# A two-layer language-model tower: where the gathered expert outputs of each sequence land

## The chip, the cores and the metric

The kernel runs on one core of a Trainium2 chip. The metric is the device time of one execution in microseconds. Before the change it is 443.67 us, the median of 3 runs (443.1 to 444.18).

## The reference, cut to what matters

Four sequences of 512 tokens go through an embedding, an attention and a feed-forward layer (layer 0), a second attention and a mixture of experts (layer 1). The end of the last layer is what the change touches:

```python
probs = jax.nn.softmax(xf @ gate_w, axis=-1)
dispatch_w, expert_idx = jax.lax.top_k(probs, 2)
combine = jnp.sum(jax.nn.one_hot(expert_idx, E) * dispatch_w[..., None], axis=1)
for e in range(8):
    h = jax.nn.gelu(xf @ w1[e] + b1[e], approximate=False)
    y = h @ w2[e] + b2[e]
    out = out + combine[:, e:e + 1] * y
return x + out.reshape(B, S, D)          # D = 128, hidden width 512
```

## The kernel before, in words

Everything is fp32. A sequence is 4 tiles of 128 tokens by 128 channels; the residual stream of all 16 tiles stays in SBUF (`h`). The kernel computes an expert only for the tokens that chose it. POOL scatters each token's row to its two experts' regions in DRAM (`dealt`), SP loads full tiles of 128 rows of one expert back, PE multiplies them, SP stores the results (`experts_out`), and POOL gathers for each token its two result rows, which DVE adds to `h` with their weights.

Work is cut into sections with a letter, a number and a phase, written X5.0 or K30.3. T, A, B, C, O are embedding and first attention of a sequence, D, H, E its first feed-forward layer, F the preparation of the second attention (linear layers, cumulative decays by scans on DVE), G its 16 blocks, I normalisation and gating, R ranking and scattering, Z the tables of tiles (group 0: sequences 0 to 2, group 1: half of sequence 3). V loads expert weights. X loads a batch of up to 4 dealt tiles, Q transposes it. K is one of 42 tiles of tokens (0 to 30 group 0, 31 to 41 group 1): K.0 on DVE copies the expert's two weight matrices to `w1s` and `w2s` (L1708, L1710; three buffers each), K.1 is the up matmul (L1049), K.2 GELU on ACT (L1262), K.3 the down matmul (L1057), K.4 the copy out of PSUM on DVE (L1713). W stores a batch of results (L574; W0 to W7 group 0, W8 to W10 group 1). J computes the last half of sequence 3 densely, for all 8 experts: J.0 up (L1012), J.1 GELU (L1272), J.2 down (L1020), J.3 add on DVE (L1614). Y0.0 on POOL gathers the result rows of a sequence (`section_Y`, L731; 8 gathers of 128 rows, 4 for sequence 3), Y.1 on DVE adds them (L1725), U stores a sequence to `out` (L588).

Each engine runs its own list of sections from the table `ORDER`, in exactly that order; semaphores alone tie the lists together. So a section that waits holds up all that stands behind it on its engine. PSUM has 8 banks; 7 of them go round as a ring in the order of PE's table, and each matmul group waits until the bank's last content has been read (`room`).

All gathers of Y land in one buffer, `yg`, which is laid over `qkv` of the first attention. So `section_Y` waits for the last matmul that reads `qkv` (C.pe.kv of sequence 3) and for the last add of the sequence before:

```python
wait(pool, "C.pe.kv", B - 1)
wait(pool, "Y.dve.b3", b - 1)
```

The end of DVE's list is `... K35.0 K36.0 Y0.1 K33.4 K34.4 K37.0 K38.0 K39.0 K35.4 K36.4 J2.3 J3.3 K40.0 Y1.1 K37.4 K41.0 K38.4 K39.4 K40.4 K41.4 J4.3 Y2.1 J5.3 J6.3 J7.3 Y3.1`.

Of the kernel before, what the change touches and what calls it, by code (L numbers as in the profile page):

```python
# [5 lines left out]
ALU = mybir.AluOpType  # L6
# [8 lines left out]
B, S, D = 4, 512, 128  # L15
T = S // P
# [15 lines left out]
LEAD = 3  # L32
# [92 lines left out]

ORDER = {
    "sp": (
        "V0.0 V1.0 V2.0 V3.0 V4.0 V5.0 V6.0 V7.0 X0.0 X1.0 X2.0 X3.0 X4.0 X5.0 X6.0 X7.0 X8.0 X9.0 X10.0 W0.0 "
        "W1.0 W2.0 W3.0 W4.0 W5.0 W6.0 W7.0 W8.0 W9.0 U0.0 U1.0 W10.0 U2.0 U3.0"),
    "pool": (  # L130
# [20 lines left out]
    "act": (  # L151
# [12 lines left out]
    "dve": (  # L164
# [16 lines left out]
}  # L181


def lm_tower(nc, a, out):
# [5 lines left out]
    with ctx:  # L190
# [11 lines left out]
        def wait(eng, step, b):  # L202

            if b >= 0:
                eng.wait_ge(sem[step.rsplit(".", 1)[0]], count(step, b))
# [93 lines left out]
        la = sb("la", [P, PAIRS, S])  # L299
# [54 lines left out]
        blk = sb("blk", [P, D + HEADS0])  # L354

        qkv = sb("qkv", [P, T, 3 * D + 1])
        yg = qkv[:].rearrange("p t c -> p (t c)")[:, 0:2 * T * D].rearrange("p (k t c) -> p k t c", k=2, t=T)
        sq = sb("sq", [P, T, 2 * D])
        amp = sq
        n2 = few("n2", [P, 4, T * 16])  # L360
# [13 lines left out]
        vv = sb("vv", [P, T, HEADS1 * HD1])  # L374
        lb = sb("lb", [P, PAIRS, S])
        kk, qq = la, lb
        zeros = lb[:].rearrange("p a b -> p (a b)")

        big = sb("big", [P, 2 * E * FF])
# [215 lines left out]
        def _(pool):  # L595
# [125 lines left out]
            def section_Y(b, ph):  # L721
                if ph == 0:
                    g = b // LEAD
                    wait(pool, "Z.dve.pi", g)
                    pool.wait_ge(s_ys[g], 16 * sum(x[0] == g for x in BATCHES))
                    wait(pool, "C.pe.kv", B - 1)
                    wait(pool, "Y.dve.b3", b - 1)
                    for t in range(PART[b]):
                        for k in range(2):
                            at = b % LEAD * T + t  # L730
                            pool.indirect_dma_start(  # L731
                                yg[:, k, t, :], None, ys[g],
                                bass.IndirectOffsetOnAxis(ap=posi[g][:, k, at:at + 1], axis=0)).then_inc(s_yg[b], 16)

            each("pool", {"A": section_A, "B": section_B, "O": section_O, "D": section_D, "H": section_H,
# [544 lines left out]
        def _(dve):  # L1280
# [434 lines left out]
            def section_Y(b, ph):  # L1715
                if ph == 1:
                    dve.wait_ge(s_yg[b], 16 * 2 * PART[b])
                    wait(dve, "R.dve.w", b)
                    wait(dve, "I.dve2.h", b)
                    for t in range(PART[b]):  # L1720
                        hb = h[:, b * T + t, :]
                        for k, name in enumerate("ab"):
                            if k:
                                wait(dve, "Y.dve.a%d" % t, b)
                            did(dve.scalar_tensor_tensor(hb, yg[:, k, t, :], wts[b // LEAD][:, b % LEAD * T + t, k:k + 1], hb, ALU.mult, ALU.add),  # L1725
                                "Y.dve.%s%d" % (name, t), b)

            each("dve", {"T": section_T, "A": section_A, "B": section_B, "C": section_C, "O": section_O,
# [86 lines left out]
```

## Time and profile before

| | before |
|---|---|
| median of 3 runs | 443.67 us (443.1 to 444.18) |
| the profiled execution | 443.62 us, span 441.5 us |
| mean granted TensorE clock | 0.956 |
| PE busy | 388.5 us (88%) |
| DVE busy | 311.1 us (70%) |
| ACT busy | 213.0 us (48%) |
| POOL busy | 135.9 us (31%) |
| gathers of expert outputs, POOL L731 | 28, mean 964 ns |

The busy shares are means over the whole span: the first 100 us, the end and a short stretch near 280 us leave PE idle, the rest is full. Engines are told apart as PE (matmul), PEld (its weight loads), DVE, ACT, POOL and SP; a `q` behind a name is the engine's queue of commands. In a timeline the idle time of the engine before an instruction stands in brackets, with what ended it. A row that groups several matmuls of one kind (x8) shows the time from the first to the modelled end of the last, which overlaps the next group a little.

### The profile page before, as it was taken

What the parts mean: (1) busy time and instruction counts of PE and PEld (TensorE: products, weight loads), DVE (VectorE), ACT (ScalarE), POOL (GpSimd) and SP (SyncE); (2) the same over time, 40 slices, a digit from 0 to 9 for tenths busy, and PEclk for the clock granted to TensorE, in tenths of its full rate; (3) what the DMA queues carried; (4) which work ended last, traced back from release to release, by engine and by line L of the source; (5) the groups of instructions that cost most, each with busy time, mean ns of one, the idle gap of its engine ahead of it and who ended that gap; (6) DMA issues with size and microseconds to landing.
All of it is one profiled execution on the core that took longest, in us unless ns stands there. A gap on an engine that the chain in (4) does not pass through costs nothing.

```text
span 441.5 us, 8913 instructions
## 1 busy us (share of the span) xinstructions
PE 388.5 (88%) x2864; PEld 305.2 (69%) x2864; DVE 311.1 (70%) x989; ACT 213.0 (48%) x456; POOL 135.9 (31%) x139
## 2 busy tenths in 40 slices
PE   2557859998999999999999999689999999999590
PEld 1334738575549875598655884368999999998590
DVE  1478798788999867999799659994377655517332
ACT  1228474953663743722346227213679466774230
POOL 6771214152403012014146027350011100065443
PEclk9996697999999999999999999899999999999896
DMA  5899500000000000000047000012220141111232
GB/s 157 321 377 423 240 0 2 1 1 0 1 1 1 1 1 1 2 1 2 0 143 286 2 1 31 19 48 57 60 57 25 50 132 49 45 49 55 62 94 71
DMA packets 24021, 31.71 MB, mean 72 GB/s; under 512 B 4377, under 2 KB 18720, under 8 KB 22696
## 3 DMA queue, kind: packets, MB, share of 16 engines
q1 hardware_dynamic: 21416, 25.63, 16.5%
q0 software_dynamic: 2560, 5.52, 4.4%
q8 instruction: 23, 0.38, 0.3%
q14 instruction: 22, 0.18, 0.1%
HBM read 18.16 MB, written 12.98 MB: 71 GB/s over the span
## 4 chain that ended last, share of the span: by engine, by line
PE 53%; DVE 17%; issue 14%; POOL 7%; DMA 5%; ACT 3%; POOLq 0%; DVEq 0%
PE bank L923 5%; POOL qkv L731 5%; PE bank L952 4%; PE bank L975 4%; PE bank L936 3%; PE bank L890 3%; PE bank L870 3%; PE bank L884 3%; PE bank L960 3%; PE bank L1049 2%; PE bank L968 2%; PE bank L917 2%; PE bank L908 2%; DMA qkv<-experts_out,arena 2%; DVE h L1725 2%
## 5 line engine op out<-in xcount | busy, mean ns | idle before, releaser
L1262 ACT ACTIVATE arena<-bank,arena 128x128 f32<-128x128 f32 x168 | 47.9, 370 | 40.1 <-PE bank L1049 39.9
L1057 PE MATMUL bank<-w2s,arena 128*128 128x128 f32 x336 | 46.0, 282 | 0.7 <-DVE fs L1713 0.7
L731 POOL DMA_INDIRECT qkv<-experts_out,arena x28 | 27.0, 964 | 63.6 <-issue 48.5
L1057 PEld LDWEIGHTS bank<-w2s,arena 128*128 128x128 f32 x336 | 42.4, 197 | 1.3 <-DVE fs L1713 0.9
L717 POOL DMA_INDIRECT dealt<-xy,arena x28 | 29.2, 1042 | 32.7 <-DVE arena L1649 25.2
L923 PE MATMUL bank<-xT_f,wq 128*128 128x512 f32 x64 | 30.5, 621 | 0.7 <-DVE vv L1508 0.7
L1710 DVE COPY w2s<-big 128x512 f32 x42 | 18.4, 437 | 16.2 <-PE bank L1057 16.1
L1708 DVE COPY w1s<-big 128x512 f32 x42 | 17.9, 426 | 14.2 <-PE bank L1049 9.8
L1540 DVE TENSOR_TENSOR arena<-bank,causal 128x512 f32<-128x512 f32 x32 | 20.3, 682 | 8.1 <-PE bank L936 8.1
L923 PEld LDWEIGHTS bank<-xT_f,wq 128*128 128x128 f32 x64 | 12.3, 198 | 15.3 <-issue 12.7
L1725 DVE SCALAR_TENSOR_TENSOR h<-qkv,arena,h 128x128 f32<-128x128 f32 x28 | 9.0, 349 | 19.5 <-DMA qkv<-experts_out,arena 19.1
L1049 PE MATMUL bank<-arena,w1s 128*128 128x128 f32 x160 | 21.3, 277 | 0.0
L1519 DVE TENSOR_TENSOR_SCAN lb<-la 128x512 f32<-128x512 f32 x16 | 20.5, 1283 | 0.0
L708 POOL TENSOR_TENSOR arena<-arena 128x8 f32<-128x8 f32 x4 | 6.8, 1690 | 41.9 <-DVE arena L1554 41.9
L1049 PEld LDWEIGHTS bank<-arena,w1s 128*128 128x128 f32 x160 | 19.4, 192 | 0.3 <-issue 0.2
L1215 ACT ACTIVATE arena<-bank 128x512 f32<-128x512 f32 x12 | 7.0, 596 | 24.9 <-PE bank L944 24.9
L689 POOL TENSOR_TENSOR arena<-arena 128x4 f32<-128x4 f32 x4 | 4.2, 1061 | 47.5 <-DVE arena L1299 47.5
L1220 ACT ACTIVATE arena<-bank 128x512 f32<-128x512 f32 x16 | 9.5, 596 | 18.5 <-PE bank L960 17.3
L936 PE MATMUL bank<-lb,la 64*128 64x128 f32 x256 | 18.3, 284 | 0.0
L952 PE MATMUL bank<-arena,vv 128*64 128x128 f32 x256 | 17.5, 279 | 0.9 <-DVE arena L1540 0.9
L599 POOL DMA_INDIRECT arena<-in_tables,idx x16 | 16.5, 1031 | 5.8 <-issue 4.4
L936 PEld LDWEIGHTS bank<-lb,la 64*128 64x128 f32 x256 | 15.5, 187 | 2.3 <-issue 1.5
(280 smaller groups left out, 1000.3 us busy)
## 6 DMA issues: line engine op xcount, KB each, us to landing
dealt<-lb SPq DMA_DIRECT2D x7, 1024.0 KB, 13.3
big<-in_tv SPq DMA_DIRECT2D x2, 2048.0 KB
big<-in_ew SPq DMA_DIRECT2D x16, 256.0 KB, 5.9
arena<-dealt SPq DMA_DIRECT2D x20, 64.0 KB, 1.8
experts_out<-arena SPq DMA_DIRECT2D x5, 256.0 KB, 3.0
wq<-in_wq SPq DMA_DIRECT2D x1, 1024.0 KB, 18.1
out<-h SPq DMA_DIRECT2D x4, 256.0 KB, 3.0
u<-dealt SPq DMA_DIRECT2D x8, 64.0 KB, 1.9
```

The source lines that it names most:

```text
L717: pool.indirect_dma_start(xs[b // LEAD], bass.IndirectOffsetOnAxis(ap=goal[b][:, k, t:t + 1], axis=0), xy[b % 2][:, t, :], None).then_inc( ...
L731: pool.indirect_dma_start(yg[:, k, t, :], None, ys[g], bass.IndirectOffsetOnAxis(ap=posi[g][:, k, at:at + 1], axis=0)).then_inc(s_yg[b], 16)
L923: did(pe.matmul(p[:], wq[:, at * 512 + j * P:at * 512 + (j + 1) * P], xT_f[:], start=True, stop=True), "F.peq.%s%d" % (name, j), b)
L936: last = pe.matmul(half[m][:, j * P:(j + 1) * P], kk[rows, j, tk], qq[rows, j, tk], start=True, stop=True)
L952: last = pe.matmul(p[m * HD1:(m + 1) * HD1, j * P:(j + 1) * P], vv[:, c, (2 * j + m) * HD1:(2 * j + m + 1) * HD1], sim[k][:, m, j, :], sta ...
L1049: last = pe.matmul(p[:, c * P:(c + 1) * P], w1s[n % WAYS][:, c * P:(c + 1) * P], tiles(g, j, 1)[:, 0, :], start=True, stop=True)
L1057: last = pe.matmul(p[:, 0:D], hid[n % 2][:, c * P:(c + 1) * P], w2s[n % WAYS][:, c * D:(c + 1) * D], start=(c == 0), stop=(c == FC - 1))
L1262: last = act.activation(hid[n % 2][:, c * P:(c + 1) * P], of("K.up", n)[:, c * P:(c + 1) * P], ACT.Gelu, bias=eb1[:].rearrange("p e c -> p ...
L1519: did(dve.tensor_tensor_scan(lb[:, j, :], la[:, j, :], la[:, j, :], 0.0, ALU.add, ALU.bypass), "F.dves.sum%d" % j, b)
L1540: did(dve.tensor_tensor(sim[n % 2][:, m], of("G.qk%d" % m, n)[:].rearrange("p (a b) -> p a b", a=PAIRS), causal[:].unsqueeze(1).to_broadca ...
L1708: did(dve.tensor_copy(w1s[n % WAYS][:], big[:, bass.ds(e * FF, FF)]), "K.dve.w1", n)
L1710: did(dve.tensor_copy(w2s[n % WAYS][:], big[:, bass.ds(e * FF + E * FF, FF)]), "K.dve.w2", n)
```

## The change

`yg` becomes a list of four buffers, one for each sequence. Sequence 0 keeps the place in `qkv`; 1 and 2 get the two halves of `vv` (the values of the second attention), 3 gets half of `la` (its keys). POOL no longer waits for the adds of the sequence before. Sequence 0 waits for C.pe.kv as before, the others for the last output projection of the second attention (G.pe3.out of block 15). DVE reads `yg[b]`. All five tables of `ORDER` are made anew: each engine has the same sections as before, in another order.

```diff
-        yg = qkv[:].rearrange("p t c -> p (t c)")[:, 0:2 * T * D].rearrange("p (k t c) -> p k t c", k=2, t=T)
+        yg = [x.rearrange("p (k t c) -> p k t c", k=2, t=T) for x in (
+            qkv[:].rearrange("p t c -> p (t c)")[:, 0:2 * T * D], vv[:].rearrange("p t c -> p (t c)")[:, 0:2 * T * D],
+            vv[:].rearrange("p t c -> p (t c)")[:, 2 * T * D:], la[:].rearrange("p a b -> p (a b)")[:, 0:2 * T * D])]
...
-                    wait(pool, "C.pe.kv", B - 1)
-                    wait(pool, "Y.dve.b3", b - 1)
+                    if b == 0:
+                        wait(pool, "C.pe.kv", B - 1)
+                    else:
+                        wait(pool, "G.pe3.out", B * T - 1)
...
-                                yg[:, k, t, :], None, ys[g],
+                                yg[b][:, k, t, :], None, ys[g],
...
-                            did(dve.scalar_tensor_tensor(hb, yg[:, k, t, :], wts[b // LEAD][:, b % LEAD * T + t, k:k + 1], hb, ALU.mult, ALU.add),
+                            did(dve.scalar_tensor_tensor(hb, yg[b][:, k, t, :], wts[b // LEAD][:, b % LEAD * T + t, k:k + 1], hb, ALU.mult, ALU.add),
```

Of the tables, the parts that the prediction speaks of, old and new:

```diff
     "sp": (
-        ... X5.0 X6.0 X7.0 X8.0 X9.0 X10.0 W0.0 W1.0 ... W8.0 W9.0 U0.0 U1.0 W10.0 U2.0 U3.0
+        ... X5.0 W0.0 W1.0 X6.0 X7.0 W2.0 X8.0 X9.0 X10.0 W3.0 ... W9.0 W10.0 U0.0 U1.0 U2.0 U3.0
     "pe": (
-        ... F0.3 O2.4 F0.7 E1.0 F0.15 F0.23 F0.31 E1.1 F0.13 F0.21 F0.29 F0.5 F0.37 E1.3 G0.2 G1.2 G0.0 ...
+        ... F0.3 O2.4 F0.7 F0.15 F0.23 F0.31 F0.13 E1.0 E1.1 F0.21 F0.29 F0.37 F0.5 G0.0 E1.3 G1.0 G0.2 ...
-        ... G11.8 R1.1 F3.3 F3.7 ... F3.37 G12.2 G13.2 G12.0 G12.5 G14.2 G13.0 G13.5 G12.4 ...
+        ... R1.1 G10.4 I1.9 ... G11.8 F3.3 I1.11 F3.7 ... F3.37 I2.9 G12.2 G13.2 G12.0 I2.11 G13.0 G12.5 G14.2 G12.4 ...
-        ... K13.3 K15.1 Q6.0 ...
+        ... K13.3 K14.1 K15.1 Q6.0 Q7.0 ...
-        ... Q8.0 K23.3 ... K29.3 K31.1 K30.3 K32.1 K31.3 Q9.0 Q10.0 K33.1 K32.3 K34.1 J2.0 J3.0 K33.3 K35.1 K34.3
-        K36.1 J2.2 J3.2 K35.3 K36.3 K37.1 K38.1 J4.0 K37.3 K39.1 K38.3 J5.0 K40.1 K39.3 K41.1 K40.3 K41.3 J4.2 J6.0
-        J5.2 J7.0 J6.2 J7.2
+        ... K29.3 Q8.0 Q9.0 K30.3 K31.1 Q10.0 J2.0 K32.1 J3.0 J2.2 K31.3 K33.1 K32.3 K34.1 K33.3 K35.1 K34.3 K36.1
+        K35.3 K37.1 K36.3 K38.1 K37.3 K39.1 J3.2 K38.3 K40.1 K39.3 K41.1 K40.3 J4.0 J5.0 K41.3 J4.2 J5.2 J6.0
+        J7.0 J6.2 J7.2
     "act": (
-        T0.1 T0.4 T0.6 T1.1 B0.0 B0.2 T1.4 B0.4 B0.6 T1.6 T2.1 C0.1 T2.4 B1.0 B1.2 T2.6 B1.4 O0.3 T3.1 B1.6 ...
+        T0.1 T0.4 T0.6 T1.1 T1.4 B0.0 B0.2 B0.4 B0.6 T1.6 T2.1 C0.1 B1.0 T2.4 B1.2 B1.4 T2.6 T3.1 O0.3 B1.6 ...
     "dve": (
-        ... A1.0 T2.2 C0.1 A1.4 T3.0 B1.1 B1.3 C0.3 B1.5 O0.0 T3.2 A2.0 B1.7 ...
+        ... A1.0 T2.2 T3.0 A1.4 C0.1 B1.1 B1.3 C0.3 B1.5 O0.0 T3.2 A2.0 B1.7 ...
-        ... F3.38 I2.12 Z0.0 G12.1 ...
+        ... F3.38 Z0.0 G12.1 I2.12 ...
-        ... K36.0 Y0.1 K33.4 K34.4 K37.0 K38.0 K39.0 K35.4 K36.4 J2.3 J3.3 K40.0 Y1.1 K37.4 K41.0 K38.4 K39.4 K40.4
-        K41.4 J4.3 Y2.1 J5.3 J6.3 J7.3 Y3.1
+        ... K30.4 K32.0 K33.0 K34.0 K35.0 J2.3 K36.0 K31.4 K32.4 K33.4 K34.4 K37.0 K38.0 K35.4 K39.0 Y0.1 K40.0
+        K36.4 K37.4 K38.4 K41.0 K39.4 J3.3 K40.4 K41.4 Y1.1 J4.3 Y2.1 J5.3 J6.3 J7.3 Y3.1
```

## Rows read from the trace of the kernel before

**Rows 1.** spans and granted clock: span in us, mean TensorE clock

```profile
core 0: 441.5 us, clock 0.956
```

**Rows 2.** waits from 380 us: waiter <- releaser, total us, times, longest

```profile
DVE h L1725 <- DMA qkv<-experts_out,arena: 19.1, 4, 5.6
...
POOL qkv L731 <- DVE h L1725: 15.1, 3, 5.1
...
PE bank L1049 <- DVE w1s L1708: 4.6, 1, 4.6
```

**Rows 3.** timeline, gathers and sums: start, duration us, engine, what, [idle before <-releaser]

```profile
385.94 0.99 POOL L731 DMA_INDIRECT qkv<-experts_out,arena  x1 [41.20 <-issue]
...
394.90 0.95 POOL L731 DMA_INDIRECT qkv<-experts_out,arena  x1 [0.31 <-issue]
...
397.37 2.69 DVE L1725 SCALAR_TENSOR_TENSOR h<-qkv,arena,h 128x128 f32<-128x128 f32 x8 [4.36 <-DMA qkv<-experts_out,arena]
...
400.45 0.43 DVE L1708 COPY w1s<-big 128x512 f32 x1
...
400.83 1.21 POOL L731 DMA_INDIRECT qkv<-experts_out,arena  x1 [4.99 <-DVE h L1725]
...
436.89 1.39 DVE L1725 SCALAR_TENSOR_TENSOR h<-qkv,arena,h 128x128 f32<-128x128 f32 x4 [4.98 <-DMA qkv<-experts_out,arena]
```

**Rows 4.** windows: length, busy PE PEld DVE ACT POOL, clock, DMA share, GB/s

```profile
382.70:400.00 17.30, 16.89 (x137) 16.28 (x135) 6.43 (x20) 10.65 (x33) 7.77 (x8) 1.00 0.15 43
...
400.00:416.00 16.00, 11.13 (x80) 10.18 (x80) 8.49 (x28) 6.03 (x20) 8.00 (x9) 1.00 0.18 51
...
416.00:431.30 15.30, 15.18 (x104) 14.60 (x104) 5.60 (x20) 5.96 (x16) 8.11 (x9) 0.89 0.39 108
...
431.30:441.50 10.20, 0.00 (x0) 0.00 (x0) 1.92 (x6) 0.00 (x0) 3.10 (x4) 0.62 0.23 63
```

**Rows 5.** timeline where group 0's last tile leaves

```profile
382.90 0.29 DVE L1713 COPY fs<-bank 128x128 f32<-128x128 f32 x1 [0.76 <-PE bank L1057]
...
383.22 0.36 SPq L574 DMA_DIRECT2D experts_out<-fs  x1
```

**Rows 6.** chain of waits, the expert stage: start, duration us, what

```profile
334.23 0.89 PE bank L1049 x8
...
335.12 1.73 PE bank L1012 x8
```

**Rows 7.** timeline of the front, DVE and PE

```profile
57.26 1.21 DVE L1366 TENSOR_REDUCE arena<-sq 128x64 f32<-128x1024 f32 x1
...
67.22 1.23 DVE L1388 TENSOR_TENSOR fs<-sq,fs 128x1024 f32<-128x1024 f32 x1
...
83.85 3.64 PE L870 MATMUL bank<-big,arena 128*32 128x512 f32 x32
```

**Rows 8.** timeline, DVE reading the bank of q0

```profile
125.73 0.74 DVE L1526 SCALAR_TENSOR_TENSOR lb<-bank,arena,lb 128x512 f32<-128x512 f32 x1
```

**Rows 9.** timeline of sequence 3's second attention, PE and DVE

```profile
264.17 0.64 PE L900 MATMUL bank<-ident,xn_f 128*128 128x128 f32 x4
...
290.13 0.68 DVE L1604 TENSOR_TENSOR h<-h,bank 128x512 f32<-128x512 f32 x1
...
297.14 1.09 PE L952 MATMUL bank<-arena,vv 128*64 128x128 f32 x16 [0.93 <-DVE arena L1540]
```

**Rows 10.** PE's longest waits from 110 to 380 us: total us, times, longest

```profile
PE bank L995 <- DVE arena L1601: 3.1, 1, 3.1
...
PE bank L944 <- DVE la L1530: 1.1, 1, 1.1
```

**Rows 11.** timeline, SP's loads of dealt rows; DVE's copy of K7

```profile
297.84 22.30 SPq L569 DMA_DIRECT2D arena<-dealt  x20
...
331.60 0.48 DVE L1713 COPY arena<-bank 128x128 f32<-128x128 f32 x2
```

**Rows 12.** timeline, POOL's slowest indirect DMA

```profile
284.94 1.62 POOL L717 DMA_INDIRECT dealt<-xy,arena  x1 [6.37 <-DVE arena L1649]
```

More of the change, by code:

```diff
@@ L127 @@
     "sp": (
-        "V0.0 V1.0 V2.0 V3.0 V4.0 V5.0 V6.0 V7.0 X0.0 X1.0 X2.0 X3.0 X4.0 X5.0 X6.0 X7.0 X8.0 X9.0 X10.0 W0.0 "
-        "W1.0 W2.0 W3.0 W4.0 W5.0 W6.0 W7.0 W8.0 W9.0 U0.0 U1.0 W10.0 U2.0 U3.0"),
+        "V0.0 V1.0 V2.0 V3.0 V4.0 V5.0 V6.0 V7.0 X0.0 X1.0 X2.0 X3.0 X4.0 X5.0 W0.0 W1.0 X6.0 X7.0 W2.0 X8.0 X9.0 "
+        "X10.0 W3.0 W4.0 W5.0 W6.0 W7.0 W8.0 W9.0 W10.0 U0.0 U1.0 U2.0 U3.0"),
     "pool": (
[2 rows of a table removed]
[2 rows of a table added]
         "F3.3 I2.1 R1.3 R2.3 I3.1 R3.3 Y0.0 Y1.0 Y2.0 Y3.0"),
```

90 rows, old and new, of the table ORDER are left out of this document.

## The prediction

> **What bounds the kernel now.** I read the span and clock first: 441.5 us at a mean granted clock of 0.956 [rows 1]; the same execution took 443.62 us, so 2.12 us lie outside the span. It stands 0.05 us under the median of 443.67 us, so the sum below is made against 443.62 and needs no correction.
>
> Next, the waits of the last 61 us [rows 2]. POOL waits 15.1 us in three pieces for the weighted sums of line 1725, and DVE waits 19.1 us in four pieces for gathers to land. That is a ring: one buffer `yg` serves all four sequences, so the gathers of sequence b+1 (POOL) start only when step Y1 of sequence b (DVE) has read it. The timeline shows one turn [rows 3]: first gather at 385.94, eighth at 394.90, DVE adds from 397.37 to 400.06, next gather at 400.83. From the eighth gather to the next sequence's first are 400.83-394.90 = 5.93 us, where a gather otherwise follows the last in 1.25 to 1.28 (7 intervals in 8.96 us). Three turns lose 3 x (5.93-1.28) = 14 us.
>
> TensorE is the other half. It is busy 16.89 of 17.3 us, then 11.13 of 16.0, then 15.18 of 15.3 at a clock of 0.89 [rows 4], and ends at 431.3. The middle hole is PE waiting 4.6 us for a `w1s` copy [rows 2] that stands behind Y1 in DVE's queue, itself waiting for a gather. So the new end is not found by subtracting 14 us: when the ring is gone, PE's own work is late next, and I rebuild the tail from that.
>
> **The change, part by part.**
>
> *Start of the tail.* The last tile of group 0, K30, is copied out at 382.90 and its store goes out on SP at 383.22 [rows 5]; the gathers start at 385.94, 3.0 us after the copy. K30's down matmuls ended 0.2 before it, at 382.70. In the new PE table the same work precedes K30.3 but for K31.1 (out, 0.89) and Q9.0 (in, 0.44), so K30.3 ends 0.45 earlier, at 382.25, and the first gather starts at 385.5.
>
> *PE's remaining work.* After K30.3 the new table has 11 K.up and 11 K.down, each 0.89, and six J.up at 1.73 [rows 6]; six J.down with 16 matmuls of K's shape each, twice 0.893, 1.79; and one Q10 of about 0.35. Sum: 22 x 0.893 + 6 x 1.73 + 6 x 1.79 + 0.35 = 41.1 us. Without a stall PE ends at 423.4, against 431.3. The clock was 1.00 in the first stretch and 0.89 after the hole [rows 4]; without the hole I take 1.00.
>
> *Does DVE stall it?* I walked DVE's new list against PE's. Y0.1 comes when K39.0 is copied, about 399.9; the gathers landed at 385.5 + 7 x 1.28 + 2.5 = 397.0 (2.5 is 397.37-394.90), so it waits for nothing, and takes 2.69 [rows 3] until 402.6. Behind it stand K40.0 (needed by K40.1 at 404.9, ready 403.0) and K41.0 (needed 406.7, ready 405.6). Both have over 1 us to spare: no stall. If the gathers came 2 us later than 399.9, this cover is gone.
>
> *POOL.* The three waits for Y.dve.b3 go; the wait for G.pe3.out is met with G15.8, ahead of K2.3 in PE's order and so before the matmuls of rows 6, and costs nothing. 24 gathers at up to 1.28 put the last start of sequence 2 at 385.5 + 23 x 1.28 = 414.9, landed 417.4. K41.3 ends at 412.8 (423.4 less 2 J.up, 4 J.down, 3.46 + 7.16 = 10.6), its store lands about 415.9. Sequence 3's four gathers start then and land at 422.3.
>
> *End.* DVE: Y1.1 413.1 to 415.8, J4.3, Y2.1 417.4 to 420.1, J5.3, J6.3, then J7.3, which needs PE's last matmul, to 424.1. Y3.1 takes 1.39 to 425.5. From the end of that step to the span's end are now 441.5-438.28 = 3.2 us [rows 1, 3]. New span: 428.7. The tail gives 441.5-428.7 = **-12.8 us**. On SP, W10 moves ahead of U0 and U1, whose waits for Y then hold nothing up.
>
> *The tables ahead of the tail* also change, with the same instructions. I followed what differs.
> - Front: DVE does T3.0 before A1.4, not between A1.4 and B1.1. The reduction of B1.1, now at 57.26 [rows 7] and kept from its input, can go 1.9 us earlier. The scalar work T2.6 and T3.1 in between leaves about 0.9 of it at step B1.7 (67.22). T1.4, placed ahead of B0.0 on ACT, delays sequence 0 by about 0.3. PE becomes dense at 83.85 [rows 7], and all that stands behind it moves by the rest: **-0.6**.
> - F of sequence 0: F0.13 now comes before E1.0. With a ring of seven banks, the matmul k1 of F0.21 takes the bank of q0, which DVE reads at 125.73 (0.74 us) [rows 8]. PE, dense here before, reaches it at about 124.6 and waits: **+1.2**. I found no such case for the other three sequences.
> - F of sequence 3: I1.11 (0.9 us) leaves the work ahead of F3.3, which starts at 264.17, and I2.12 (0.68) moves behind G12.1 on DVE [rows 9]. G12.1 ends 1.6 earlier; its waiter G12.4 (297.14) can follow, but 1.09 of matmuls (G13.5) are then still to do: **-0.5**.
> - What I didn't follow: bounds 0 and 4.2, the two longest PE waits of the stretch from 110 to 380 [rows 10], should new ones of that size appear. PE showed almost none in its dense stretch, so I take the value near zero: **+0.6**. Below zero there is little, as PE is full there.
> - SP: X6 and X7 now stand behind W1. Twenty such loads take 22.30 us [rows 11], so seven take 8, after W1, which follows the copy of K7 at 331.6; they land at 342, and Q6.0 comes near 350. Nothing is lost.
>
> Sum: 443.62 - 12.8 - 0.6 + 1.2 - 0.5 + 0.6 = **431.5 us**.
>
> *Gathers beside DVE copies.* The gather at 400.83, with a DVE copy that began at 400.45 and others behind it, took 1.21 us where the one at 394.90 took 0.95 [rows 3]; I allowed for that with 1.28. The Trainium skill ("SBUF — State Buffer", "SBUF: two separate sides") speaks against the change: a DMA issued by GpSimd can't write its descriptors while VectorE runs a copy from SBUF to SBUF, which holds the shared port. The copies of `w1s` and `w2s` are such. By its figures ("A bandwidth-pool intuition that's wrong") a DMA of 620 ns becomes one of 3100 ns; if every gather did, its stream would end past 470 us. That is an estimate from the page; the rows show a tenth of that effect.
>
> **Rivals.**
> 1. *The tables cost more.* The dense stretch is given up in places for a short tail. Price: the 4.2 us bound in place of 0.6, 435.1 us; the range for it is 433.5 to 437.5. For: the bank wait above. Against: no dependency changed there. Chance 0.20.
> 2. *The ring goes, but DVE still waits at Y0.1 or PE at a late copy*, as now [rows 2]. One 4.6 us wait returns: 436.1 us, and up to the bounds of "same". Chance 0.05.
> 3. *Slower: the gather stream becomes the bound.* If the port collisions hit each gather, it costs what the slowest indirect DMA of this kernel cost, 1.62 us [rows 12], plus the 0.30 between two. Then 28 in a row end at 385.5 + 27 x 1.92 + 2.5 = 439.8, and the time is 439.8 + 1.39 + 3.2 + 2.12 = 446.5 us. It exceeds the present time from a spacing of 1.81 us on. Most gathers show 1.25. Chance 0.03.
> 4. *The change doesn't do what it says*: ys[0] or the DVE places of Y1 hold the gathers anyway. Then about 443 us. Against: rows 2 name DVE as the releaser three times. Chance 0.02.
> 5. *More gain*: the front's 1.9 us arrives in full and nothing is lost: 443.62-12.8-1.9-0.5 = 428.4 us. Chance 0.12.
>
> The forecast (429.5 to 433.5) has 0.58. The range from 428.0 to 437.0 holds it, nearly all of rivals 1 and 5 and half of 2. Within 0.2% (0.9 us, about what a measurement of this kernel can tell from no change) lies rival 4 alone; slower is rival 3 alone. Faster 0.95, same 0.02, slower 0.03.
>
> **What would show it.** Right: 24 gathers in one run of 1.25 to 1.3 us from about 385 to 415, no POOL wait for line 1729; PE busy over 98% from 382 to 423 at a clock of 1.00; Y0.1 without a DMA wait; the last chain running through PE and J, not POOL. A PE wait of some 1 us at 124 shows the bank step, a start of PE's dense work near 83 the front. Wrong: gathers of 1.6 us or more; a PE wait over 2 us after 382; K30.3 later than 384, which would put the loss in the tables.

## The result, and the profile after

On the chip of the first comparison the changed kernel took 431.89 us (430.96 to 432.71) beside 443.43 us for the kernel before: a ratio of 0.9733, interval 0.9708 to 0.9758. The prediction was 431.5 us. On another chip it was the other way round, 461 us against 446, and kernels with the same gathers lost on two more of the four chips of the later groups. Both are told here, the first result first.

The profiled execution took 430.96 us with a span of 429.2 us at a mean clock of 0.972. The windows of the tail (us, then busy time and instruction count of each engine, clock, DMA share, GB/s):

```profile
380.00:400.00 20.00, 20.00 (x167) 19.59 (x166) 8.58 (x27) 13.70 (x43) 10.92 (x11) 1.00 0.25 70
400.00:420.00 20.00, 20.00 (x152) 19.18 (x151) 11.84 (x39) 10.51 (x31) 15.21 (x16) 1.00 0.36 103
```

Against [rows 4], PE has no hole and the clock stays at 1.00. The waits of the last 60 us (engine, what waited, releaser: us in total, times, longest), and the timeline's gathers and adds (start, us, engine, line, operation, idle before):

```profile
POOL vv L735 <- issue: 4.9, 16, 0.3
DVE h L1729 <- DMA vv<-experts_out,arena: 1.0, 1, 1.0
DVE h L1729 <- DMA la<-experts_out,arena: 0.7, 1, 0.7
```

```profile
385.73 0.98 POOL L735 DMA_INDIRECT qkv<-experts_out,arena  x1 [34.64 <-issue]
387.02 0.96 POOL L735 DMA_INDIRECT qkv<-experts_out,arena  x1 [0.31 <-issue]
...
400.38 2.68 DVE L1729 SCALAR_TENSOR_TENSOR h<-qkv,arena,h 128x128 f32<-128x128 f32 x8
...
413.37 2.70 DVE L1729 SCALAR_TENSOR_TENSOR h<-vv,arena,h 128x128 f32<-128x128 f32 x8
...
420.09 0.99 POOL L735 DMA_INDIRECT la<-experts_out,arena  x1 [0.30 <-issue]
...
423.76 0.61 DVE L1618 SCALAR_TENSOR_TENSOR h<-bank,arena,h 128x128 f32<-128x128 f32 x2 [1.18 <-PE bank L1024]
425.11 1.39 DVE L1729 SCALAR_TENSOR_TENSOR h<-la,arena,h 128x128 f32<-128x128 f32 x4 [0.74 <-DMA la<-experts_out,arena]
```

The three POOL waits for DVE are gone, and of the 19.1 us that DVE waited for gathers [rows 2] 1.7 are left. All 28 gathers stand in one run from 385.73 to 420.09, where the ring of [rows 3] stretched them to 434.37. Y0.1, at 400.38, waits for no DMA. PE's last product is done at 423.7, but the chain that ended last runs through POOL's gathers and the landing of the last one, and not through PE as the prediction's sign for "right" wanted:

```profile
420.09 5.00 DMA la<-experts_out,arena
```

### The profile page after: what moved, and what is told of

Its sections match the earlier page's. It is cut to its first block, busy times and chain, and to the rows that moved or that the text cites. A ratio compares the mean times of both kernels' runs of the same rounds, so it can differ in the third digit from the quotient of the medians.

```text
span 429.2 us, 8910 instructions
## 1 busy us (share of the span) xinstructions
PE 381.6 (89%) x2864; PEld 300.8 (70%) x2864; DVE 312.9 (73%) x989; ACT 214.2 (50%) x456; POOL 137.4 (32%) x139
## 4 chain that ended last, share of the span: by engine, by line
PE 55%; DVE 17%; issue 12%; POOL 8%; ACT 4%; DMA 3%; POOLq 0%; DVEq 0%
PE bank L1053 8%; PE bank L1061 8%; PE bank L927 3%; PE bank L979 3%; PE bank L956 3%; PE bank L894 3%; PE bank L940 2%; POOL vv L735 2%; PE bank L964 2%; DMA arena<-in_tables,idx 2%; PE bank L972 2%; POOL arena L601 2%; PE bank L874 2%; PE bank L1016 2%; PE bank L813 2%
## 5 line engine op out<-in xcount | busy, mean ns | idle before, releaser
L1061 PE MATMUL bank<-w2s,arena 128*128 128x128 f32 x336 | 44.2, 275 | 0.0
L719 POOL DMA_INDIRECT dealt<-xy,arena x28 | 31.4, 1120 | 33.7 <-DVE arena L1653 26.4
L1061 PEld LDWEIGHTS bank<-w2s,arena 128*128 128x128 f32 x336 | 41.0, 192 | 0.1
L1714 DVE COPY w2s<-big 128x512 f32 x42 | 18.0, 428 | 19.1 <-PE bank L1061 18.9
L1523 DVE TENSOR_TENSOR_SCAN lb<-la 128x512 f32<-128x512 f32 x16 | 19.5, 1218 | 2.0 <-ACT la L1205 2.0
L1219 ACT ACTIVATE arena<-bank 128x512 f32<-128x512 f32 x12 | 7.0, 594 | 25.5 <-PE bank L948 25.5
L735 POOL DMA_INDIRECT qkv<-experts_out,arena x8 | 7.7, 964 | 36.8 <-issue 36.8
L735 POOL DMA_INDIRECT vv<-experts_out,arena x16 | 15.5, 971 | 4.9 <-issue 4.9
L979 PE MATMUL bank<-wo,arena 128*128 128x128 f32 x128 | 17.0, 280 | 0.0
```

The source lines that it names most:

```text
L719: pool.indirect_dma_start(xs[b // LEAD], bass.IndirectOffsetOnAxis(ap=goal[b][:, k, t:t + 1], axis=0), xy[b % 2][:, t, :], None).then_inc( ...
L735: pool.indirect_dma_start(yg[b][:, k, t, :], None, ys[g], bass.IndirectOffsetOnAxis(ap=posi[g][:, k, at:at + 1], axis=0)).then_inc(s_yg[b] ...
L979: last = pe.matmul(p[:, 0:D], oc[k][:, j, :], wo1[:, j, :], start=(j == 0), stop=(j == PAIRS - 1))
L1061: last = pe.matmul(p[:, 0:D], hid[n % 2][:, c * P:(c + 1) * P], w2s[n % WAYS][:, c * D:(c + 1) * D], start=(c == 0), stop=(c == FC - 1))
L1523: did(dve.tensor_tensor_scan(lb[:, j, :], la[:, j, :], la[:, j, :], 0.0, ALU.add, ALU.bypass), "F.dves.sum%d" % j, b)
```

## Experiments

### The four pieces apart, and the first surprise

Two kernels separate buffers and tables, one keeps the old tables up to the tail, and one puts copies beside the gathers.

```
e1: ORDER of the kernel before; buffers and waits of the change
e2: ORDER of the change; one buffer and wait(pool, "Y.dve.b3", b - 1) of the kernel before
e3: as e1, with the new order of PE from behind K29.3, ACT from behind K30.2, DVE from behind K30.0, SP from W3.0
```

> The four buffers with the order tables of the kernel before. Theory (the ring of gather and add was the loss, and the buffers alone remove it): the first 12 gathers run as before, the next 8 follow them without a break, so Y1.1 starts near 407.5 us instead of 412.4, Y2.1 and Y3.1 wait for TensorE's last products instead of for gathers, and TensorE's work sets the end. The stall of TensorE at the weight copy behind Y0.1 in the old VectorE order stays, so the end lies 1 to 3 us behind that of the new tables: 433.7 us (432.0 to 435.5). Rival (the new tables carry the gain, the buffers only permit them): within 2 us of the kernel before, 441.5 to 443.5 us.

> The new order tables with the one buffer and the waits of the kernel before. Theory: the ring returns, and since the new VectorE order puts the adds of sequences 0 and 1 later, it is closed later than in the kernel before: the gathers of sequence 1 from about 403.8 us, Y1.1 near 415.3, the gathers of sequence 2 from 418.7, Y2.1 near 430.1, those of sequence 3 from 433.5, end near 446.5 us (444.5 to 448), slower than the kernel before by some 3 us. Rival (the tables carry the gain): 432 to 436 us.

> The four buffers with the old order tables up to the TensorE turn K29.3 and the VectorE turn K30.0, and the new order behind them. Theory: the new tables ahead of the tail are worth 0.2 to 0.5 us, since the 1.2 us they gain by 83 us are given back by 105 us; so 431.9 to 432.5 us, within 0.2% of the changed kernel. Rival (the front's gain of 1.2 us is kept to the end and the tail alone explains less): 433.1 us or more.

The fourth:

```
+    for x in [w1m[:]] + [wq[:, i * 512:(i + 1) * 512] for i in range(4)] + [
+            wo1[:].rearrange("p a b -> p (a b)"), bv1[:], w1t[:]] if n == 41 else []:
+        dve.tensor_copy(x, w2m[:])
     wait(dve, "K.pe2.down", n)
```

> The changed kernel with eight more VectorE copies of 128x512 float32 from one SBUF buffer to dead ones, ahead of the last result copy K41.4, where VectorE sat idle for 4.05 us (409.1 to 413.2) beside the gathers of sequence 2. They compute nothing that is used. By the rows of this kernel (gathers beside such copies took 1.04 to 1.26 us against 0.95) each of the three or four gathers beside them takes 0.1 to 0.3 us longer, Y2.1 starts up to 1 us later, the end moves by 0 to 0.8 us. By the rule that a gather can't write descriptors while such copies run, no gather would get through between 409.1 and 412.7: the gathers behind are all 3 us later, sequence 3's last is issued at about 423 us and the end is 2.5 to 3 us later, 434.5 us.

Measured, beside 447.43 us for the kernel before: e1 458.97 us (ratio 1.0228, 1.0185 to 1.0271), e2 456.59 (1.0209, 1.0152 to 1.0266), e3 459.58 (1.0248, 1.0212 to 1.0284), e6 462.37 (1.0318, 1.0284 to 1.0351). No expectation held, and the split between buffers and tables can't be read from these four, because all of them show something that neither first trace has. In e1, PE's timeline, with the gathers running from 385.6 on:

```profile
398.51 0.37 PE L1023 MATMUL bank<-big,ht 128*128 128x128 f32 x1 [1.06 <-issue]
399.91 0.37 PE L1023 MATMUL bank<-big,ht 128*128 128x128 f32 x1 [1.03 <-issue]
400.63 0.37 PE L1023 MATMUL bank<-big,ht 128*128 128x128 f32 x1 [0.34 <-issue]
...
406.97 0.37 PE L1023 MATMUL bank<-big,ht 128*128 128x128 f32 x1 [1.75 <-issue]
409.77 0.37 PE L1023 MATMUL bank<-big,ht 128*128 128x128 f32 x1 [2.43 <-issue]
...
418.90 0.37 PE L1023 MATMUL bank<-big,ht 128*128 128x128 f32 x1 [0.33 <-issue]
419.59 4.00 PE L1023 MATMUL bank<-big,ht 128*128 128x128 f32 x18 [0.33 <-issue]
```

These matmuls take 0.11 us each elsewhere (16 in 1.79). Here they start 0.7, 1.4, 2.1 or 2.8 us apart, in steps of 0.7, and wait for nothing that the profile shows. At 419.59, 4.8 us after the start of the 24th gather (414.82), they run back to back again, at first in 0.22 us each, since the granted clock had fallen to 0.50 while PE stood. The effect is no matter of unbroken gathers alone: e2 keeps the ring and its pauses, and still lost 9 us. In its trace the products that PE makes beside the first eight gathers (389.45 to 398.27) reach DVE and ACT only at 400.4 to 401.2 us; Y0.1, which stands behind K39.0 in the new order, comes at 410.91, and the next gathers start only at 414.37. In e6 the added copies ran only from 441.3 to 444.1, when no gather ran, so it says nothing on copies beside gathers, and that question got no answer.

### Is it the kernel or the chip?

> The changed kernel itself once more, beside the kernel before. In the four kernels of the first group the signal of a TensorE product that was done by 391 us reached VectorE and ScalarE 7 to 27 us late while GpSimd's gathers ran, and their times were 455 to 462 us. If that belongs to the chip or the moment and not to those four kernels, this one shows it too: about 456 to 459 us, with late signals between 390 and 420 us. If it belongs to the four kernels (an order or an instruction count), this one takes 431 to 433 us on the same chip.

> The kernel before itself, for its trace on the chip of the others: if the late signals belong to the chip, they show between 386 and 400 us here too, and the time is about 447 us, as it was beside the first group; if not, 443 to 444 us and no signal more than 0.5 us behind its product.

The unchanged texts of both kernels, on another chip: the changed kernel took 460.95 us (460.07 to 462.24), the kernel before 445.97 us, ratio 1.0339 (1.0311 to 1.0366); the single profile of the kernel before 445.64 us. So it isn't the four kernels. The same program that took 431.9 us takes 29 us more on this chip (456 to 459 were expected). The windows for the 35 us of the gathers, first in the first trace of the changed kernel, then here:

```profile
385.00:420.00 35.00, 35.00 (x276) 33.91 (x275) 18.16 (x58) 20.99 (x64) 26.13 (x27) 1.00 0.30 86
385.00:420.00 35.00, 15.31 (x105) 14.44 (x103) 4.46 (x12) 7.57 (x23) 23.10 (x24) 0.73 0.18 52
```

PE, busy throughout in the first trace, is busy 15.31 us. Its timeline shows how:

```profile
392.82 1.06 PE L1061 MATMUL bank<-w2s,arena 128*128 128x128 f32 x8
393.71 1.06 PE L1053 MATMUL bank<-fs,w1s 128*128 128x128 f32 x8
394.61 1.06 PE L1061 MATMUL bank<-w2s,arena 128*128 128x128 f32 x8
395.50 1.06 PE L1053 MATMUL bank<-fs,w1s 128*128 128x128 f32 x8
397.39 0.43 DVE L1714 COPY w2s<-big 128x512 f32 x1 [8.71 <-remote]
402.36 1.14 ACT L1266 ACTIVATE arena<-bank,arena 128x128 f32<-128x128 f32 x4 [9.37 <-remote]
403.64 2.04 PE L1061 MATMUL bank<-w2s,arena 128*128 128x128 f32 x8 [7.09 <-ACT arena L1266]
...
412.90 0.43 DVE L1714 COPY w2s<-big 128x512 f32 x1 [14.30 <-remote]
417.88 0.94 POOL L735 DMA_INDIRECT vv<-experts_out,arena  x1 [0.30 <-issue]
422.72 2.22 ACT L1266 ACTIVATE arena<-bank,arena 128x128 f32<-128x128 f32 x8 [19.22 <-remote]
424.01 2.05 PE L1061 MATMUL bank<-w2s,arena 128*128 128x128 f32 x8 [16.61 <-ACT arena L1266]
```

DVE's `w2s` copy at 397.39 waits for the product of PE at 392.82 alone, which its record ends at 393.9: 3.5 us late. The copy at 412.90 waits for the product at 394.61: 17 us late. ACT's step at 402.36 waits for the product recorded at 393.71, 7.6 us late, and one of the two at 422.72 for that at 395.50, 26 us late. Then everything runs again, 4.8 us after the start of the 24th gather, as in e1. PE comes back at the lower of its two clocks (granted 0.50 from 404 to 424 us): the product at 424.01 takes 2.05 us, where one at full clock takes 1.06. "remote" stands where the page finds no releaser on this core. Whether PE itself was slow, as in e1, or only its signals, can't be told: matmul ends are modelled. The gathers themselves are not slower: 0.96 us in mean, 0.97 in the first trace. The last four, which start at 447.24 after a pause of 28 us, hold nothing up that shows.

The kernel before suffers less. Its profile on this chip has a span of 443.5 us against 441.5. Its windows on the chip of the first result, then here:

```profile
384.00:400.00 16.00, 15.59 (x125) 14.98 (x124) 5.79 (x19) 9.99 (x30) 7.77 (x8) 1.00 0.16 46
384.00:400.00 16.00, 14.12 (x101) 13.69 (x100) 5.28 (x16) 10.31 (x30) 7.78 (x8) 0.93 0.16 46
```

Its ring cuts the gathers into groups of eight, and PE runs on in the pauses: back to back again from 397.53, 2.4 us after the start of the eighth gather. Its PE ends at 435.4 us, 4 later than on the first chip, and the span is 2 us longer.

### What holds PE up: an indirect gather, or any transfer?

```
-    pool.indirect_dma_start(
-        yg[b][:, k, t, :], None, ys[g],
-        bass.IndirectOffsetOnAxis(ap=posi[g][:, k, at:at + 1], axis=0)).then_inc(s_yg[b], 16)
+    row = (2 * at + k) * P
+    pool.dma_start(yg[b][:, k, t, :], ys[g][row:row + P, :]).then_inc(s_yg[b], 16)
```

> The changed kernel with each of its 28 gathers made a plain transfer of the same size: 128 rows of 512 B that lie one after the other in the experts' output, on the same GpSimd queue, into the same buffers, with the same waits. The rows summed are therefore the wrong ones; all else is computed. Theory (the descriptors of indirect gathers hold up TensorE's signals on the chips where the change lost): the signals are on time and the kernel takes 432 us or less there, some 14 us under the kernel before. Rival (any transfer of these bytes and landings does it): late signals as with the gathers, 455 to 461 us. Where a chip shows no late signals at all, both expect 428 to 432 us.

433.55 us, ratio 0.9699 (0.9643 to 0.9755), on a third chip, in a group whose other two kernels, e45 and e9 below, have indirect gathers and took 461 us. PE in the same stretch:

```profile
385.00:420.00 35.00, 35.00 (x282) 34.07 (x281) 18.43 (x57) 19.94 (x62) 15.06 (x27) 1.00 0.30 84
```

As many bytes and packets in the same buffers from the same queue do no harm; with the 28 transfers indirect, kernels that differ besides in two or four moves take some 28 us more on this chip (461.67 and 461.08 against 433.55). The theory held, if 1.6 us above its 432, and the rival (any transfer does it) fell. One difference is left: without a wait the plain transfers follow one another at 0.53 us, not 1.25, and occupy POOL for 0.54 us each, not 0.95. Plain transfers at nearly the gathers' pace were run only on a chip of the first kind (below). x1 keeps the indirect transfers at the start and the 28 scatters, 16 of which stand between 268 and 296 us; its first read starts at 388.04 where the first trace of the changed kernel has its first gather at 385.73. Between 276 and 297 us its PE falls from 0.4 to 2.5 us behind that trace, and in the repeat of the changed kernel from 0.9 to 3.0 us. Most of this is no mark of the chip: p4 below, with the same tables on a chip of the first kind, falls from 0.4 to 1.7 us there. Some 0.8 us are left that may belong to the scatters' effect on PE; 28 of the repeat's 29 us arise in the tail.

### Two moves, and two more at the end

```
e45: pe   "... F0.31 E1.0 E1.1 F0.13 F0.21 ..."      pool "A2.1 D0.1 A2.3 D0.3 B2.5 A3.1 ..."
e9:  e45, sp "... U1.0 U3.0 U2.0"                    dve  "... J5.3 J6.3 Y3.1 J7.3"
```

> The changed kernel with two moves in its order tables: TensorE's turn F0.13 behind E1.1 (the bank wait of 0.78 us at 125.3 us should go), and GpSimd's B2.5 behind D0.3 (VectorE's operations beside three GpSimd additions in a row should take 0.2 and 0.7 us again, not 0.9 and 1.7, and TensorE's wait of 0.8 us at 93.3 us should go). If both gains last, 1.2 to 1.6 us less than the changed kernel on the same chip; if VectorE's stretch of 264 to 297 us takes them back, 0 to 0.3 us less.

> The two moves of the kernel beside it and two more at the end: the store of sequence 2's result behind that of sequence 3, and VectorE's Y3.1 ahead of J7.3. In the changed kernel the last gather landed 5.0 us after its issue, against 2.4 to 2.7 for the others, with the 256 KB store of sequence 2 issued 0.2 us behind it. Theory (the store delays it): the last gather lands at about 422.8 us, Y3.1 runs before TensorE's last product is done, J7.3 ends about 425.0 instead of Y3.1 at 426.5, so 1 to 1.5 us less than with two moves; from that the two stores together at the end can take back up to 1 us. Rival (the store has nothing to do with it): Y3.1 still waits until 425, J7.3 follows it, 0.6 us more than with two moves.

461.67 us (ratio 1.0323, 1.0265 to 1.0382) and 461.08 us (1.0303, 1.0233 to 1.0373), beside 448.65 us for the kernel before (445.5 to 454.4): no gain over the changed kernel (460.95 us, on another chip of the kind; it wasn't timed on this one). Each local effect did occur in e45. PE has no bank wait, and the wait for E0.3 is gone. DVE, without three POOL additions in a row beside it, does the second operation in its usual time (first fence the recorded changed kernel, second e45):

```profile
82.62 1.28 POOL L659 TENSOR_TENSOR sq<-kab,sq 128x512 f32<-128x512 f32 x1 [10.41 <-ACT kab L1134]
83.01 0.93 DVE L1384 TENSOR_SCALAR arena<-arena 128x32 f32<-128x32 f32 x1
83.86 1.29 POOL L652 TENSOR_TENSOR h<-h,bo 128x512 f32<-128x512 f32 x1
83.98 1.72 DVE L1388 TENSOR_TENSOR lnu<-lnu,arena 128x512 f32<-128x512 f32 x1
```

```profile
83.75 1.29 POOL L658 TENSOR_TENSOR sq<-kab,sq 128x512 f32<-128x512 f32 x1 [6.92 <-ACT kab L1133]
84.14 0.94 DVE L1383 TENSOR_SCALAR arena<-arena 128x32 f32<-128x32 f32 x1
85.11 0.69 DVE L1387 TENSOR_TENSOR lnu<-lnu,arena 128x512 f32<-128x512 f32 x1
```

But the step came 1 us later, and behind both moves, at 255 us, PE's 1,500th matmul starts 0.1 us later than in the repeat of the changed kernel. In e9 nothing waits for the last gather; from J7.3's start to the end of the span are 4.3 us against 4.7, so 0.4 us came from the end, not the 1 to 1.5 of the theory. Whether the store delayed that gather stays open: in the repeat, with the store in its old place, no such wait shows either.

### Buffers and tables apart, without indirect gathers

```
     pool.dma_start(... ys[g][row:row + P, :]).then_inc(s_yg[b], 16)
+    pool.value_load(eid[g][0:1, 0:1], min_val=0, max_val=E - 1)
```

> The kernel before (one buffer, old tables) with plain transfers of the same size in place of its 28 gathers, as in x1, and one register load of GpSimd behind each, so that they follow one another at about 1.2 us, as the gathers do (1.25 us). Wrong rows are summed; all else is computed. The ring of add and transfer stays; landing takes 2.2 us instead of 2.5 and the spacing is a little shorter: 440 to 444 us, 6 to 10 us more than x1 (433.55 us). If it is under 436 us, the ring was not what held the kernel before.

> The same replacement and pace with four buffers and the old order tables. Theory (the ring was the loss and the buffers remove it; TensorE's wait for the weight copy behind Y0.1 stays): 0.5 to 3 us more than x1, 434 to 436.5 us. Rival (the new tables carry the gain, the buffers only permit them): within 3 us of the first kernel of this group.

> The same replacement and pace with the new order tables and one buffer. Theory: the ring closes later than with the old tables, since Y0.1 and Y1.1 stand later in VectorE's order: 1 to 4 us more than the first kernel of this group. Rival (the new tables carry the gain): within 3 us of x1.

Beside 443.74 us for the kernel before: p2 436.00 us (0.9813, 0.9779 to 0.9847), p3 431.65 (0.9730, 0.9703 to 0.9757), p4 440.98 (0.9932, 0.9906 to 0.9957). The adds in DVE's timeline, p2, p3 and p4 in turn:

```profile
396.23 2.69 DVE L1724 SCALAR_TENSOR_TENSOR h<-qkv,arena,h 128x128 f32<-128x128 f32 x8 [1.87 <-DMA qkv<-experts_out]
409.43 2.69 DVE L1724 SCALAR_TENSOR_TENSOR h<-qkv,arena,h 128x128 f32<-128x128 f32 x8 [2.62 <-DMA qkv<-experts_out]
422.47 2.69 DVE L1724 SCALAR_TENSOR_TENSOR h<-qkv,arena,h 128x128 f32<-128x128 f32 x8 [3.25 <-DMA qkv<-experts_out]
430.82 1.39 DVE L1724 SCALAR_TENSOR_TENSOR h<-qkv,arena,h 128x128 f32<-128x128 f32 x4 [2.79 <-DMA qkv<-experts_out]
```

```profile
395.19 2.69 DVE L1728 SCALAR_TENSOR_TENSOR h<-qkv,arena,h 128x128 f32<-128x128 f32 x8 [1.97 <-DMA qkv<-experts_out]
405.58 2.68 DVE L1728 SCALAR_TENSOR_TENSOR h<-vv,arena,h 128x128 f32<-128x128 f32 x8
416.20 2.68 DVE L1728 SCALAR_TENSOR_TENSOR h<-vv,arena,h 128x128 f32<-128x128 f32 x8
425.01 1.38 DVE L1728 SCALAR_TENSOR_TENSOR h<-la,arena,h 128x128 f32<-128x128 f32 x4
```

```profile
402.03 2.68 DVE L1724 SCALAR_TENSOR_TENSOR h<-qkv,arena,h 128x128 f32<-128x128 f32 x8
415.07 2.68 DVE L1724 SCALAR_TENSOR_TENSOR h<-qkv,arena,h 128x128 f32<-128x128 f32 x8
427.28 2.69 DVE L1724 SCALAR_TENSOR_TENSOR h<-qkv,arena,h 128x128 f32<-128x128 f32 x8 [9.01 <-DMA qkv<-experts_out]
435.70 1.39 DVE L1724 SCALAR_TENSOR_TENSOR h<-qkv,arena,h 128x128 f32<-128x128 f32 x4 [3.73 <-DMA qkv<-experts_out]
```

p2 missed its range of 440 to 444, and it stands at the 436 us under which the ring was to be ruled out. Its trace shows the ring all the same: POOL waits 14.8 us in three pieces for the adds, 15.1 in the kernel before. The time came out low because the transfers followed one another mostly at 0.98 us, not 1.2, and with a ring each such interval counts. In the profiled execution (437.52 us, 6.1 under 443.62) the 24 intervals inside the groups take 25.3 us instead of 30.5, the three turns between them 16.4 instead of 17.9, the last landing 0.4 less, and the first transfer starts 1.15 us later. p3 gets 4.3 us from the buffers alone and ends with PE: its last add waits for no DMA. It was expected at 434 to 436.5: the wait of PE behind Y0.1 did not come, since reads 0.98 us apart land 2 us sooner. p4, the new tables with one buffer, is 5.0 us slower than p2 (expected 1 to 4): Y0.1 stands 6 us later in DVE's order, and the ring closes behind it. So with plain transfers the buffers gain by themselves, and the new tables cost time without them. What the tables add to four buffers wasn't measured where signals are on time, with plain transfers or with gathers; p3, with the old tables, is as fast as the changed kernel was (431.65 and 431.89 us). That the buffers carry the 11.5 us with indirect gathers too is argued from this and from the waits that went.

In these traces the steps of DVE and ACT in the tail start within 0.15 us of the PE product that they wait for, as in the first trace, and none waits for "remote", though the 28 scatters and the start are indirect here too, and the kernel before took 443.7 us: this chip behaves as that of the first result, and the other three are a second kind, where the kernel before took 446 to 449.

## Why the prediction was right, and where it was wrong

*On the first kind of chip*, by the profiled executions (443.62 to 430.96 us, -12.66; forecast -12.1):

- Start of the tail. K30's copy is at 382.70 us, 0.2 earlier than before. The regrouping ahead of K30.3 was to give 0.45 of that, so the other edits ahead of the tail cost 0.25 us, against +0.7 in my sum (-0.6+1.2-0.5+0.6). The first gather is at 385.73; with that +0.7, which I added only at the end, I had it at 386.2. The front gave twice the gain that I took (PE dense at 82.64, -1.2 against [rows 7]), but 0.8 of it was lost at 93 us: the POOL additions of the fence above run beside two DVE operations, ACT waits 1.73 us for the second and PE 0.8 us for ACT. The bank wait was 0.78 us, not 1.2. G12.4 starts 0.29 us earlier, not 0.5. New waits were few: from 110 to 370 us PE waited 8.1 us, before 7.1.
- PE's remaining work. From K30.3's end (382.50, 0.2 before its copy) to the end of PE's last product (423.7) are 41.2 us; forecast 41.1. The list of matmul groups at the unstalled rate was right.
- No stall at Y0.1: right (400.38; forecast 399.9, or 400.6 with the +0.7; no wait).
- Spacing: 27 intervals in 34.36 us, 1.27 each (1.28 taken): 1.25 mostly, up to 1.48 beside copies.
- End. Wrong by 2.8 us in one row: sequence 3's gathers landed at 425.1, not 422.3. They started as forecast (416.29 for 415.9), but the last took 5.0 us to land, where the median of the 28 is 2.5. It cost 0.7 us, since J7.3 ends at 424.4 in any case. From Y3.1's end to the span's end were 2.7 us, not 3.2, and 1.7 us lay outside the span, not 2.1. Tail and outside together: -12.9 against -12.8. That this agrees so well is luck in part: 0.7 us too little for the last landing stands against 0.9 us too much for the rest of the end.
- Rival 3 (the port). Three gathers beside a copy took 1.04 to 1.18 us against 0.95, as [rows 3] had said; others beside one took 0.95. By the Trainium skill ("SBUF — State Buffer", "SBUF: two separate sides") the shared port is held for a whole instruction, so a gather would wait for the copy that holds it. The copies here last 0.43 us; the prediction had put the Trainium skill's figure of 3100 ns in their place, and the 0.23 us that the slowest lost don't contradict the rule. In the other direction the row is large: DVE's 0.69 us operation took 1.72 beside POOL's additions.

*On the second kind* it was wrong by 29 us, with the wrong sign. The step that failed is "Without a stall PE ends at 423.4": in the repeat of the changed kernel PE ends at 454.8. It assumed that a gather costs PE nothing but the wait for its data. Both rows that supported it, [rows 4] and [rows 6], come from a chip where that holds. No row of the trace before could show the other kind, but none excluded it: rival 3 let the gathers slow each other, and none of the rivals let them slow PE. Taking the pauses out of the gather stream, the gain on one kind of chip, is a loss on the other (e1, buffers alone: 11.5 us); the new tables lose there as well, even with the pauses kept (e2: 9 us).

Not settled: why the chips differ. All timed executions here were also recorded, and on the second kind the trace holds fewer semaphore updates (4,216 in the repeat of the changed kernel, 5,015 in its first trace), missing in the stretches with indirect transfers. In x1 they are missing only at the start and at the scatters (4,540 are left), and on the chip of p2 to p4 none are (5,018 to 5,022). So the recording may take part, and the loss may be one of recorded executions alone: none was timed without it. Nor is it known what in an indirect transfer holds PE up.

No version that computes the right sums was found to beat both kernels on both kinds of chip. Not tried: fewer indirect transfers, or pauses between them, with four buffers. e2 warns that pauses alone may not do.

## What to carry to other kernels

Where a wait ring holds a tail, don't subtract its waits: rebuild the tail from the remaining work of the next engine; that sum, 41.1 us, was right to 0.1. Give the buffers first and reorder after, since an order made for free buffers costs time with one (p4: 5.0 us). And ask of each transfer that is made denser what runs beside it, and time the result on more than one chip: a gain of 2.7% was a loss of 3.4% elsewhere.

## What the runs showed of the hardware that was not expected

- On three of the four chips of the later groups PE nearly stands still while a run of GpSimd's indirect transfers lasts, and for some us from the start of the last (4.8 behind 24 gathers, 2.4 behind eight): matmuls spaced by 0.7 us or multiples of it (e1), and signals of finished products up to 26 us late (the repeat of the changed kernel). The same 64 KB as plain transfers had no such effect on one of these chips (x1). Whether it shows without the recording is open.
- A plain transfer of 64 KB takes POOL 0.54 us (x1, p2), an indirect gather of 128 rows 0.95 and then 0.30 to the next.
- DVE beside POOL's additions: an operation of 0.18 us took 0.93, and with a second and third addition right behind the first, one of 0.69 took 1.72. With a single addition (e45) the second took 0.69.
